# Attention with a maxima pass 20 slots ahead instead of 16, and the row of maxima sent behind exponential tile 13 instead of 17

## The chip, the cores and the metric

One core of a Trainium2 chip runs the whole program. The metric is the device time of one execution in microseconds (us), the median of several runs. TensorE is PE, VectorE is DVE, ScalarE is ACT, GpSimd is POOL, SyncE is SP. POOL, SP and ACT can issue DMAs; all of them run on the core's 16 DMA engines.

## The reference

The program embeds two inputs, runs an attention layer with quantised projections, and a mixture of eight experts. Both parts of the change lie in the attention's score, softmax and value steps:

```python
Q = (proj(q_weight, WQ, q_bias) * scaling).reshape(bsz, tgt, HEADS, HEAD_DIM)   # 32 heads of 16
K = proj(k_weight, WK, k_bias).reshape(bsz, tgt, HEADS, HEAD_DIM)
V = proj(v_weight, WV, v_bias).reshape(bsz, tgt, HEADS, HEAD_DIM)
attn = jnp.einsum('bqhd,bkhd->bhqk', Q, K)
probs = jax.nn.softmax(attn, axis=-1)
ctx = jnp.einsum('bhqk,bkhd->bqhd', probs, V).reshape(bsz * tgt, H)
```

There are 4 batches of 640 tokens and 32 heads, so 128 heads, each with a 640 x 640 score matrix. float32 precision is kept by splitting Q and K into three bf16 parts each; six pairs of parts of 16 rows are stacked on 96 partitions.

## The kernel before

`attend` works through 32 groups of 4 heads (group 0 to 31; in the code the group is `R * i + c` with R = 4). Every group goes through two passes over its scores.

**The first pass** finds each query's maximum. It has M1 = 26 slots. 25 of them are scores of 128 queries, one bank of 512 columns each (L1165; every fifth slot holds the last 128 keys of all four heads, L1168, four small matmuls). DVE reduces each bank to its negated maximum (L1255, L1257). The banks are three, `mbank`, so slot n waits on `s_mfree` until DVE has read the slot three back. Behind a group's last slot DVE joins the two halves (L1260, `nm`). Slot 4 of each group, TURN, is no score: it transposes the maxima of the group before (L1158), which needs that group's `nm`; DVE copies the result to `nmT` (L1242).

**Sending the row.** The second pass computes the scores the other way round, keys on partitions, and has the negated maximum added by the matmul itself: row 96 of `qs` (MROW) holds it, opposite ones in `ks`. ACT fills that row with a DMA of 5 KB (`put_max`, L1293), which waits until DVE has copied `nmT`. ACT issues it in the stream of its exponentials, behind tile PUT_AT of the group before.

**The second pass** has U2 = 25 tiles of scores (L1183, every fifth L1186), in three other banks, `sbank`. Tile 0 waits for the row's DMA (`s_nm`). ACT takes the exponential of each (L1281) into `pT`; tile n waits for the exponential three back. At the step from the fourth group of a loop round to the first of the next, two successive tiles fall on the same bank (`behind` gives a distance of 1). PE multiplies five exponential tiles at a time with the values (`add_values`, L1201), behind tiles 2, 7, 12, 17 and 22. ACT copies the finished context behind tile 3 of the next group (L1287), SP stores it (L1087).

**PE's order** is written out by hand in `group` (L1205): ahead of each second-pass tile s stands about one slot of the first pass. The list `ahead` is the rest of group g+1 from slot LEAD on, and then the first LEAD slots of group g+2. So with LEAD = 16 tiles 0 to 9 of group g go with slots 16 to 25 of g+1, and tiles 10 to 24 with slots 0 to 15 of g+2 (two at tile 24). Ahead of group 0 stand all slots of group 0 and the first LEAD slots of group 1, with no second pass beside them. In group 30, which has no g+2, a last transposition stands ahead of tile M1 - LEAD + 3.

**SP's order.** In group g SP stores group g-1's context and loads group g+3: six pieces each of `qs` and `ks` (L1079) and one `vs` (L1082, 320 KB), into one of four buffers. Slot 0 of a group waits for all 13 (`s_ld`). In the last two groups SP stores group 30's context, reloads context and sums, issues eight broadcasts of inverted sums (L167), and then stores group 31's context; the block ends when that has landed.

**POOL** meanwhile splits the experts' weights into bf16 halves, one of 24 pieces per group, from `SPLIT_PACE`: a load of 1 MB from memory (L1124), a cast, a subtraction, a store of 1 MB (L1140). The last piece is done in group 23.

Of the kernel before, what the change touches and what calls it, by code (L numbers as in the profile page):

```python
# [98 lines left out]
def early_fusion_kernel(nc, a, out):  # L99
    ctx = ExitStack()  # L100
    with ctx:
# [62 lines left out]
        def load_inverses(sp, b):  # L164
            for i in range(IT):
                at = (b * IT + i) * (HEADS // IT)
                sp.dma_start(den[:, b % 2, i], d_sum[at:at + HEADS // IT].unsqueeze(1).broadcast_to([HEADS // IT, HD, T])  # L167
                             ).then_inc(s_ctx[b], 16)

        attend(nc, a, locals())  # L170
        route(nc, a, locals())
        middle.close()
# [811 lines left out]
def attend(nc, a, g):  # L984
# [22 lines left out]
    PIECES = [(0, 512), (512, T - 512)]  # L1007
    CTX_AT = 3
    LAG = 3
    LEAD = 16  # L1010
    PUT_AT = 17
    R = 4
    NI = NG // R
    SPLIT_PACE = 5
# [1 line left out]
    with ctx:  # L1016
# [128 lines left out]
        def _(pe):  # L1145
            def first_pass(i, c, slot, static=False, turn=TURN):


                u, n, d = c % R, M1 * num(i, c) + slot, behind(first_bank, M1, c, slot)
                if not static or n >= d:  # L1150
                    pe.wait_ge(s_mfree, n - d + 1)
                out = ps[:, first_bank(c, slot)]
                if slot == turn:
                    if static and c == 0:
                        pe.transpose(out[0:GH * KT, 0:P], ident[:, 0:GH * KT], ident[:]).then_inc(s_m, 1)
                        return
                    pe.wait_ge(s_nmr, num(i, c))
                    pe.transpose(out[0:GH * KT, 0:P], nm[(c - 1) % 2][:], ident[:]).then_inc(s_m, 1)  # L1158
                    return
                if slot == 0:  # L1160
                    pe.wait_ge(s_ld[u], 16 * LOADS * (i + c // R + 1))
                qt, h = divmod(slot - (slot > TURN), U1)
                q = slice(qt * P, (qt + 1) * P)
                if h < GH:
                    mm = pe.matmul(out, qs[u][0:STACK, h, q], ks[u][0:STACK, h, 0:512], start=True, stop=True)  # L1165
                else:
                    for h in range(GH):
                        mm = pe.matmul(out[:, h * REST:(h + 1) * REST], qs[u][0:STACK, h, q], ks[u][0:STACK, h, 512:T],  # L1168
                                       start=True, stop=True)
                mm.then_inc(s_m, 1)  # L1170
# [34 lines left out]
            def group(i, c, static=False, following=2):  # L1205

                ahead = [(c + 1, slot) for slot in range(LEAD, M1)] if following >= 1 else []
                ahead += [(c + 2, slot) for slot in range(LEAD)] if following >= 2 else []
                for s in range(U2):
                    for cc, slot in ahead[s * M1 // U2:(s + 1) * M1 // U2]:  # L1210
                        first_pass(i, cc, slot)
                    if following == 1 and s == M1 - LEAD + 3:
                        first_pass(i, c + 2, 0, turn=0)
# [11 lines left out]
            for slot in range(M1):  # L1225
                first_pass(0, 0, slot, static=True)
            for slot in range(LEAD):
                first_pass(0, 1, slot, static=True)
# [44 lines left out]
        def _(act):  # L1273
# [9 lines left out]
            def copy_context(i, c):  # L1283
                u = c % 2
                act.wait_ge(s_pv, KT * (num(i, c) + 1) + 1)
                act.wait_ge(s_ost[u], 16 * (R // 2 * i + c // 2) + 1)
                act.copy(osb[u][:], pv[:, 0:T]).then_inc(s_oev, 1)  # L1287

            def put_max(i, c, at=TURN):

                u = c % 2
                act.wait_ge(s_mfree, M1 * (num(i, c) + 1) + at + 1)
                act.dma_start(qs[c % R][MROW:MROW + 1].rearrange("p h (k t) -> p (h k) t", k=KT),  # L1293
                              nmT[u][:]).then_inc(s_nm[u], 16)

            def group(i, c, first=False, put=TURN):
                for s in range(U2):
                    exps(i, c, s)
                    if s == CTX_AT and not first:
                        copy_context(i, c - 1)  # L1300
                    if s == PUT_AT and put is not None:
                        put_max(i, c + 1, at=put)
# [622 lines left out]
```

## Time and profile before

| | |
|---|---|
| median of 3 runs | 1871.68 us (1866.7 to 1874.78) |
| profiled execution | 1869.23 us, its span 1867.4 us |
| busy share of the span | PE 75%, DVE 70%, ACT 41%, POOL 27% |
| granted TensorE clock, mean | 0.859 |
| attention, first score of the first pass to last context copy | about 434 to 1076 us |
| experts, on the chain that ended last | 1375 us to the end |

A span is from the first to the last instruction of the profiled execution. "Idle before <-releaser" gives an engine's idle time ahead of an instruction and what ended it; an idle time of PE with the releaser "DMA qs<-nmT" is a second pass that waited for its row of maxima. Timelines merge instructions of one kind that follow each other; a row's length is that of their union. An engine name with a q (ACTq, SPq) is a DMA issue on that engine's instruction stream. The granted clock is 1.00 at 2.4 GHz and 0.50 at 1.2 GHz.

### The profile page before, as it was taken

What the parts mean: (1) busy time and instruction counts of PE and PEld (TensorE: products, weight loads), DVE (VectorE), ACT (ScalarE), POOL (GpSimd) and SP (SyncE); (2) the same over time, 40 slices, a digit from 0 to 9 for tenths busy, and PEclk for the clock granted to TensorE, in tenths of its full rate; (3) what the DMA queues carried; (4) which work ended last, traced back from release to release, by engine and by line L of the source; (5) the groups of instructions that cost most, each with busy time, mean ns of one, the idle gap of its engine ahead of it and who ended that gap; (6) DMA issues with size and microseconds to landing.
All of it is one profiled execution on the core that took longest, in us unless ns stands there. A gap on an engine that the chain in (4) does not pass through costs nothing. (4 is left out here: it accounts for less than half of the span.)

```text
span 1867.4 us, 30349 instructions
## 1 busy us (share of the span) xinstructions
PE 1396.8 (75%) x10245; PEld 783.8 (42%) x10245; DVE 1302.6 (70%) x2158; ACT 767.8 (41%) x1459; POOL 510.8 (27%) x325
## 2 busy tenths in 40 slices
PE   0365128746999999999999914359549999999993
PEld 0344013311433444444444301034537777777772
DVE  7976889987877888888888457885534444444441
ACT  4474002330666777777777700011203333333331
POOL 4000114653333434333200002324112333233321
PEclk9987558875999999999999965565569999999997
DMA  4002003779466676767554332001547887888865
GB/s 142 1 1 82 0 1 103 223 229 209 113 190 183 183 216 180 205 187 206 141 106 78 113 113 62 28 1 57 198 196 261 261 269 262 272 286 267 261 171 135
DMA packets 112867, 289.02 MB, mean 155 GB/s; under 512 B 19566, under 2 KB 54126, under 8 KB 102650
## 3 DMA queue, kind: packets, MB, share of 16 engines
q1 hardware_dynamic: 89154, 205.74, 35.7%
q0 software_dynamic: 22592, 79.70, 15.6%
q10 hardware_dynamic: 1056, 2.79, 0.5%
q8 instruction: 32, 0.52, 0.1%
q14 instruction: 33, 0.27, 0.0%
HBM read 201.17 MB, written 92.08 MB: 157 GB/s over the span
## 5 line engine op out<-in xcount | busy, mean ns | idle before, releaser
L1281 ACT ACTIVATE pT<-p 128x512 f32<-128x512 f32 x800 | 421.6, 607 | 173.8 <-PE p L1183 171.5
L1255 DVE TENSOR_REDUCE mxa<-p 128x1 f32<-128x512 f32 x640 | 409.3, 681 | 102.9 <-PE p L1165 102.8
L1165 PE MATMUL p<-ks,qs 96*128 96x512 bf16 x640 | 254.1, 400 | 30.8 <-DMA vs<-d_v 29.1
L1183 PE MATMUL p<-qs,ks 128*128 128x512 bf16 x640 | 246.2, 385 | 31.5 <-DMA qs<-nmT 19.9
L1201 PE MATMUL p<-pT,vs 128*32 128x128 f32 (+1 forms) x2560 | 207.5, 442 | 1.0 <-ACT pT L1281 1.0
L1786 PE MATMUL p<-x,w 128*128 128x256 bf16 x1728 | 191.6, 273 | 0.0
L1786 PEld LDWEIGHTS p<-x,w 128*128 128x128 bf16 x1728 | 169.1, 98 | 23.4
L1757 POOL DMA_INDIRECT d_acc<-yo,slot_row x54 | 86.7, 1606 | 311.5 <-DMA d_acc<-yo,slot_row 248.5
L1865 DVE SCALAR_TENSOR_TENSOR sg<-p,b,sg 128x256 f32<-128x256 f32 x108 | 52.2, 483 | 121.3 <-ACT sg L1831 121.2
L1201 PEld LDWEIGHTS p<-pT,vs 128*32 128x32 f32 x2560 | 67.1, 109 | 153.1 <-issue 110.3
L1136 POOL CAST xT<-xT 128x2048 bf16<-128x2048 f32 x24 | 45.3, 1887 | 303.4 <-PE p L1201 292.2
L1165 PEld LDWEIGHTS p<-ks,qs 96*128 96x128 bf16 x640 | 62.2, 97 | 141.4 <-DVE mxa L1255 46.6
L1831 ACT ACTIVATE sg<-p,b1s 128x256 f32<-128x256 f32 x108 | 51.2, 474 | 170.8 <-PE p L1786 170.8
L1257 DVE TENSOR_REDUCE mxb<-p 128x4 f32<-128x512 f32 x160 | 108.7, 680 | 0.4 <-PE p L1168 0.4
L1786 PE MATMUL p<-x,shared 128*128 128x256 bf16 x864 | 97.7, 276 | 0.8 <-ACT x L1823 0.8
L1138 POOL TENSOR_TENSOR xT<-xT 128x2048 bf16<-128x2048 f32 x24 | 97.7, 4072 | 2.0
L1798 PE MATMUL p<-w,y 128*128 128x512 bf16 x432 | 96.2, 379 | 0.0
L1183 PEld LDWEIGHTS p<-qs,ks 128*128 128x128 bf16 x640 | 62.6, 98 | 73.7 <-ACT pT L1281 35.5
L1836 ACT CAST y<-yf 128x256 bf16<-128x256 f32 x108 | 43.7, 404 | 117.6 <-DVE yf L1868 117.6
L1786 PEld LDWEIGHTS p<-x,shared 128*128 128x128 bf16 x864 | 85.3, 99 | 13.6 <-ACT x L1823 1.1
L1880 DVE SCALAR_TENSOR_TENSOR yo<-p,slot_prob,b2p 128x512 f32<-128x512 f32 x54 | 38.0, 746 | 65.0 <-PE p L1798 65.0
L1871 DVE TENSOR_TENSOR y<-yf,y 128x256 bf16<-128x256 f32 x108 | 46.0, 426 | 50.9 <-ACT y L1836 50.9
(335 smaller groups left out, 2189.5 us busy)
## 6 DMA issues: line engine op xcount, KB each, us to landing
w<-d_w SPq DMA_DIRECT2D x18, 2048.0 KB, 8.5
d_w<-xT POOLq DMA_DIRECT2D x24, 1024.0 KB, 6.5
shared<-d_w SPq DMA_DIRECT2D x9, 2048.0 KB, 8.2
w<-d_w SPq DMA_DIRECT2D x18, 1024.0 KB, 7.4
xT<-in_w1T POOLq DMA_DIRECT2D x16, 1024.0 KB, 10.8
qs<-d_q SPq DMA_DIRECT2D x192, 80.0 KB, 3.6
ks<-d_k SPq DMA_DIRECT2D x192, 80.0 KB, 3.6
d_v<-xT SPq DMA_DIRECT2D x20, 512.0 KB, 4.4
```

The costliest lines, as they stand in the source:

```text
L1138: pool.tensor_tensor(lo, wf[u], hi, ALU.subtract).then_inc(s_wsp, 1)
L1165: mm = pe.matmul(out, qs[u][0:STACK, h, q], ks[u][0:STACK, h, 0:512], start=True, stop=True)
L1183: mm = pe.matmul(out, ks[u][:, h, k], qs[u][:, h, 0:512], start=True, stop=True)
L1201: mm = pe.matmul(pv[rows, at:at + n], vs[u][:, kt, rows], src[:, col:col + n], start=kt == 0, stop=kt == KT - 1, tile_position=(0, 32 * h))
L1255: dve.tensor_reduce(mxa[u][:, h, qt:qt + 1], bank, AX.X, ALU.max, negate=True).then_inc(s_mfree, 1)
L1257: dve.tensor_reduce(mxb[u][:, :, qt], bank.rearrange("p (h k) -> p h k", h=GH), AX.X, ALU.max, negate=True).then_inc(s_mfree, 1)
L1281: act.activation(dst, ps[:, second_bank(c, s)], ACT.Exp).then_inc(s_p, 1)
L1757: pool.indirect_dma_start(d_acc, bass.IndirectOffsetOnAxis(slot_row[:, j:j + 1], 0), yo[j % OUTS][:], None, compute_op=ALU.add).then_inc(s ...
L1786: mm = pe.matmul(out, w[c][:, k, ws, t, cols], x[c][:, t, xs], start=t == 0 and m == 0, stop=t == IT - 1 and m == 2)
L1798: mm = pe.matmul(ps[:, 6 + q], y[c][:, t, ys, q * P:(q + 1) * P], w[c][:, 2, ws, t], start=t == 0 and m == 0, stop=t == IT - 1 and m == 2)
L1831: act.activation(sg[o % 2][:], ps[:, 2 + o, 0:UNIT], ACT.Sigmoid, scale=1.702, bias=b1s[c][:, 0, o:o + 1]).then_inc(s_sg, 1)
L1865: dve.scalar_tensor_tensor(sg[o % 2][:], gate, b1[c][:, 0, o:o + 1], sg[o % 2][:], ALU.add, ALU.mult).then_inc(s_u, 1)
```

## The change

Two constants. `LEAD`, the number of first-pass slots of group g+2 that stand in group g, goes from 16 to 20. `PUT_AT`, the exponential tile behind which ACT issues the row's DMA, goes from 17 to 13.

```diff
     CTX_AT = 3
     LAG = 3
-    LEAD = 16
-    PUT_AT = 17
+    LEAD = 20
+    PUT_AT = 13
     R = 4
```

Through LEAD the tiles 0 to 5 of group g now go with slots 20 to 25 of g+1 and tiles 6 to 24 with slots 0 to 19 of g+2. No instruction is added or removed; DVE's, SP's and POOL's own orders stay as they were.

PE, second group of the attention's loop body (c = 1), around the transposition of the maxima (L1158). L1165 and L1168 are first-pass slots, L1183 and L1186 second-pass tiles, L1201 the values; the REGISTER_ALU rows compute what a semaphore is compared with. Before, tiles 13 (row 320) to 15:

```order
316 L1201 MATMUL p<-pT,vs 32x128 x4
317 L1151 REGISTER_ALU
318 L1165 MATMUL p<-ks,qs 128x512
319 L1176 REGISTER_ALU
320 L1183 MATMUL p<-qs,ks 128x512
321 L1151 REGISTER_ALU
322 L1158 MATMUL p<-ident,nm 20x128
323 L1176 REGISTER_ALU
324 L1186 MATMUL p<-qs,ks 128x128 x4
325 L1151 REGISTER_ALU
326 L1168 MATMUL p<-ks,qs 128x128 x4
```

After, tiles 8 (row 298) to 10 (row 306):

```order
295 L1201 MATMUL p<-pT,vs 32x128 x4
296 L1165 MATMUL p<-ks,qs 128x512
297 L1176 REGISTER_ALU
298 L1183 MATMUL p<-qs,ks 128x512
299 L1151 REGISTER_ALU
300 L1165 MATMUL p<-ks,qs 128x512
301 L1176 REGISTER_ALU
302 L1186 MATMUL p<-qs,ks 128x128 x4
303 L1151 REGISTER_ALU
304 L1158 MATMUL p<-ident,nm 20x128
305 L1176 REGISTER_ALU
306 L1183 MATMUL p<-qs,ks 128x512
```

The transposition stood ahead of tile 14 and stands ahead of tile 10, one run of values (that behind tile 12) earlier.

ACT, first group of the loop body, around the row's DMA (L1293). Before, exponentials 16, 17 and 18:

```order
204 L1281 ACTIVATE pT<-p 128x512
205 L1279 REGISTER_ALU
206 L1281 ACTIVATE pT<-p 128x512
207 L1292 ISA
208 L1293 DMA qs<-nmT 1x20x128
209 L1279 REGISTER_ALU
210 L1281 ACTIVATE pT<-p 128x512
```

After, exponentials 12, 13 and 14:

```order
195 L1281 ACTIVATE pT<-p 128x512
196 L1279 REGISTER_ALU
197 L1281 ACTIVATE pT<-p 128x512
198 L1292 ISA
199 L1293 DMA qs<-nmT 1x20x128
200 L1279 REGISTER_ALU
201 L1281 ACTIVATE pT<-p 128x512
```

The ISA row is the wait for `nmT`. The DMA stood behind the last exponential ahead of a run of values and stands behind the first exponential after one.

PE ahead of group 0: slots of group 1 and the first tile of the second pass. Before:

```order
196 L1165 MATMUL p<-ks,qs 128x512 x4
197 L1168 MATMUL p<-ks,qs 128x128 x4
198 L1165 MATMUL p<-ks,qs 128x512
199 L1183 MATMUL p<-qs,ks 128x512
200 L1165 MATMUL p<-ks,qs 128x512
```

After:

```order
196 L1165 MATMUL p<-ks,qs 128x512 x4
197 L1168 MATMUL p<-ks,qs 128x128 x4
198 L1165 MATMUL p<-ks,qs 128x512 x4
199 L1168 MATMUL p<-ks,qs 128x128 x4
200 L1183 MATMUL p<-qs,ks 128x512
```

Four more slots (three on L1165, one on L1168) stand ahead of the first second-pass tile.

## Rows read from the trace of the kernel before

**Rows 1.** Stretches: length, busy PE, PEld, DVE, ACT, POOL, clock, DMA share, GB/s

```profile
500.00:600.00 100.00, 91.50 (x795) 39.69 (x795) 79.99 (x134) 67.65 (x129) 36.54 (x20) 0.98 0.68 187
...
900.00:1000.00 100.00, 98.26 (x873) 42.90 (x869) 85.06 (x146) 73.33 (x140) 6.67 (x4) 1.00 0.54 111
```

**Rows 2.** Waits of PE, 485 to 1050 us: us in total, times, longest

```profile
PE p L1183 <- DMA qs<-nmT: 16.6, 18, 2.2
PE p L1183 <- ACT pT L1281: 8.5, 34, 0.5
```

**Rows 3.** Timeline of PE, one group: start us, us, what, [idle before <-releaser]

```profile
700.28 0.39 PE L1183 MATMUL p<-qs,ks 128*128 128x512 bf16 x1 [0.47 <-DMA qs<-nmT]
...
704.02 0.38 PE L1165 MATMUL p<-ks,qs 96*128 96x512 bf16 x1
...
707.50 0.38 PE L1165 MATMUL p<-ks,qs 96*128 96x512 bf16 x1
...
710.58 0.27 PE L1158 MATMUL p<-ident,nm 128*20 128x128 f32 x1
...
712.05 0.38 PE L1183 MATMUL p<-qs,ks 128*128 128x512 bf16 x1
...
719.11 0.39 PE L1183 MATMUL p<-qs,ks 128*128 128x512 bf16 x1 [0.44 <-DMA qs<-nmT]
```

**Rows 4.** Timeline of ACT, the same group

```profile
710.78 2.06 ACT L1281 ACTIVATE pT<-p 128x512 f32<-128x512 f32 x4 [0.97 <-PE p L1183]
712.56 0.73 ACTq L1293 DMA_DIRECT2D qs<-nmT  x1
712.71 0.63 ACT L1281 ACTIVATE pT<-p 128x512 f32<-128x512 f32 x1
```

**Rows 5.** Timeline of SP, the same group, the last two loads

```profile
710.54 1.12 SPq L1079 DMA_DIRECT2D ks<-d_k  x1
711.84 0.88 SPq L1082 DMA_DIRECT2D vs<-d_v  x1
```

**Rows 6.** Timeline of POOL, the same group, the load of an expert's weights

```profile
709.76 0.78 POOL L1124 DMA_DIRECT2D xT<-in_w2T  x1
```

**Rows 7.** Tile view of vs, 485 to 1050 us, its last line

```profile
DMA to landing us min/median/max: 4.3/8.2/9.4
```

**Rows 8.** Timeline of PE, first scores of groups 1, 23, 24 and 28

```profile
481.47 0.38 PE L1183 MATMUL p<-qs,ks 128*128 128x512 bf16 x1
...
909.27 0.38 PE L1183 MATMUL p<-qs,ks 128*128 128x512 bf16 x1
...
928.45 0.39 PE L1183 MATMUL p<-qs,ks 128*128 128x512 bf16 x1 [0.47 <-ACT pT L1281]
...
1003.20 0.39 PE L1183 MATMUL p<-qs,ks 128*128 128x512 bf16 x1 [0.47 <-ACT pT L1281]
```

**Rows 9.** Timeline of PE, first scores of groups 4 and 7

```profile
542.57 0.39 PE L1183 MATMUL p<-qs,ks 128*128 128x512 bf16 x1 [2.17 <-DMA qs<-nmT]
...
603.41 0.38 PE L1183 MATMUL p<-qs,ks 128*128 128x512 bf16 x1 [1.94 <-DMA qs<-nmT]
```

**Rows 10.** Stretch behind group 4's start (columns as in Rows 1)

```profile
543.40:546.80 3.40, 3.40 (x20) 0.73 (x19) 1.10 (x2) 1.28 (x3) 0.24 (x1) 0.50 0.00 0
```

**Rows 11.** Timelines of PE, DVE and ACT ahead of the first group

```profile
458.03 0.61 PE L1165 MATMUL p<-ks,qs 96*128 96x512 bf16 x1
461.88 0.61 PE L1183 MATMUL p<-qs,ks 128*128 128x512 bf16 x1 [3.24 <-DMA qs<-nmT]
...
456.10 2.46 DVE L1255 TENSOR_REDUCE mxa<-p 128x1 f32<-128x512 f32 x4
...
452.62 1.36 ACTq L1293 DMA_DIRECT2D qs<-nmT  x1
```

**Rows 12.** Timelines of ACT and SP, last two groups

```profile
1060.18 0.69 ACT L1287 COPY osb<-p 128x640 f32<-128x640 f32 x1
...
1077.59 1.26 SPq L1087 DMA_DIRECT2D d_o<-osb  x1
```

## The prediction

> **What bounds the kernel now.** I read the view by stretches first. Between 500 and 600 us PE is busy 91.5 of 100 us, between 900 and 1000 us 98.3; DVE 80 to 85, ACT 68 to 73 [rows 1]. PE sets the pace of the attention, so the question is what its idle time waits for. The view of waits answers: from 485 to 1050 us PE stood 16.6 us in 18 waits on the DMA of the row of maxima, up to 2.2 us at a time, and 8.5 us in 34 waits on ACT's exponentials [rows 2]. The timelines then show one such wait from its cause: in group 12, which starts at 700.28, the transposition runs at 710.58 and ACT issues the DMA at 712.56; the next group's first score starts at 719.11, when the row is in [rows 3, 4]. That is 6.55 us from issue to use. SP's last two loads and POOL's 1 MB load are issued at 710.54, 711.84 and 709.76, just ahead of the row [rows 5, 6].
>
> **What a wait is really worth.** The 16.6 us can't be taken as the gain, since a group that doesn't wait meets other limits. The trace holds such groups: 24 to 27, behind POOL's last piece. They run from 928.45 to 1003.20, 74.75 us or 18.69 each, and none waits for the row [rows 8]. Groups 1 to 22 run from 481.47 to 909.27, 427.8 us or 19.45 each [rows 8]. If each took 18.69, they would take 411.2, a gain of 16.6 us. This agrees with the waits only by way of three corrections. Every fourth group starts with a wait of 0.47 us on ACT, since its tile 0 falls on the bank of the tile before [rows 8]. In four of the 18 waits (ahead of groups 4, 8, 12 and 20) the row's hides this, so 1.9 us of it stay. Behind the two longest waits, of 2.17 us and 1.94 us, the granted clock fell to 1.2 GHz for 3.4 us each; the stretch behind the first is shown [rows 9, 10]. Half speed for 3.4 us costs up to 1.7 us, so some 3.2 us come on top if these waits go. And a group that starts without a pause has DVE a little behind, which the total absorbs. 16.6 - 1.9 + 3.2 is 17.9; I take the 16.6 that the unwaiting groups give.
>
> **The change part by part.**
> *The row, four tiles earlier.* PUT_AT alone would put the DMA's wait ahead of the transposition; LEAD moves the transposition from tile 14 to tile 10, so it is still three tiles ahead of the issue. Exponentials 13 to 16 started at 710.78, and the DMA at 712.56, 0.15 us ahead of exponential 17 at 712.71, which had already been handed over [rows 4]. Behind exponential 13 the same DMA starts at about 710.78 - 0.15 = 710.63, 1.9 us earlier. The first score was ready to run 0.44 us before 719.11 [rows 3]. So an issue 1.9 us earlier covers every wait up to 1.9 us even if the way of the DMA doesn't get shorter; of the 18 only the 2.17 and the 1.94 leave a rest, 0.3 us together. It is also ahead of the 320 KB of `vs` in time, not behind it [rows 5], which should rather shorten the way. What is late next is the next group's tile 0 behind its own exponentials and DVE, the pace of groups 24 to 27. Gain 16 to 17 us.
>
> *A rule on queues.* From issue to use the row took 6.55 us beside SP's and POOL's loads [rows 3, 4]. The Trainium skill, DMA: Bandwidth & Descriptors, section "Queues, rings and completion order", has each DMA engine serve its queues in turn, packet by packet. By that the way would hang on the traffic of the moment and not on SP's backlog, and an issue 1.9 us earlier would land about 1.9 us earlier. The sum would be the same; only a way longer by 1.9 us would undo it, which is a rival below.
>
> *The cost in ACT's stream.* The issue takes 0.73 us [rows 4]. Today it stands ahead of a pause: exponential 18 waits for PE, which adds values. Behind exponential 13 it stands in a run of five. There the exponentials follow each other in (2.06 - 0.60) / 3 = 0.49 us [rows 4], 0.60 being one alone. Exponential 14 started at 711.27 and would now start behind 710.63 + 0.73 = 711.36, say 711.45, and end at 712.05. PE's tile 17 needs its bank and started at 712.05 [rows 3]. So the cost is 0 to 0.1 us a group, up to 3 us in 30. I take 1. The far bound is the issue ahead of the first group, 1.36 us [rows 11]: 0.6 us more a group, 18 us. I stay near 0.73, since that row repeats in all of the other groups.
>
> *Slot 0 of a group, four tiles earlier.* It waits for the group's loads. It stands ahead of tile 6 now, 704.02 - 700.28 = 3.74 us into the group, where it stood ahead of tile 10, at 7.22 [rows 3]. The last load of that group is issued at 711.84 and lands 8.2 us later (9.4 at most), at 720.0 [rows 5, 7]. With groups of 18.4 us slot 0 comes at 700.28 + 18.4 + 3.74 = 722.4. That leaves 2.4 us, at the longest landing 1.2. I cost it at nothing; the cover is thin, and a rival has its price.
>
> *DVE.* It joins the maxima behind slot 25, now in the run of tiles 3 to 7 and not 8 to 12. One reduction takes 0.61 us in a run (2.46 us for four, 0.68 for one alone [rows 11]), a run of five and the join 3.6 us, about what PE takes for five tiles, five slots and the values (707.50 - 704.02 = 3.48 [rows 3]). Nothing or some tenths, either way.
>
> *Ahead of group 0.* Four more slots stand there, 2.4 us at DVE's 0.61. PE idled 3.24 us there for its first row, after its last slot [rows 11]. The four slots fit in, 0 to 0.3 us. Group 30 has four slots less beside its second pass, and is held by ACT for most of its tiles: 0.3 to 0.9 us less; I take 0.4.
>
> *Behind the attention.* The end is a chain on SP: the copy of group 30's context at 1060.18, its store, the sums and their broadcasts, and group 31's store at 1077.59 [rows 12]. It starts with group 31's tile 3, so what the groups before save comes through whole. The experts' part is not touched.
>
> **The sum**, against the profiled execution's own time: 1869.2 - 16.6 (groups 1 to 22) - 0.4 (group 30) + 1.0 (ACT) = 1853.2, a gain of 16.0 us, 0.86%. The profiled execution lies 2.45 us under the median of the runs, 1871.68. Against the median: 1855.7. The forecast's own range is 1849 to 1862: the gain of 16.6 with the far corrections (17.9, 0.9 for group 30, a higher clock in group 0, some run-to-run difference) below, a third of the waits left above.
>
> **The rivals.**
> 1. *The row's landing doesn't come earlier.* If what lets it in is the moment at which SP's and POOL's traffic has gone, then an earlier issue only waits longer. For it: the way is 6.5 us beside that traffic, and the start at 719.11 is near the landing of `vs` at 720.0 [rows 3, 5, 7]. Against it: the row is 5 KB and would now stand ahead of `vs`. With half of the gain lost the time is 1863, with all of it 1871.
> 2. *ACT's issue blocks its run.* SP's issues stretch to 1.12 us and 0.88 us just when the row would now be issued [rows 5]. If ACT's stretches alike, to 1.36 us [rows 11], tile 17 comes 0.6 us late in each of 30 groups: 18 us against 17, 1873. Against it: today's issue overlaps SP's stretched one of 711.84 to 712.72 and takes 0.73 [rows 4, 5].
> 3. *Slower: slot 0 waits for its loads.* Place: PE, ahead of tile 6. It decides from a landing of over 8.2 + 2.4 = 10.6 us. Each us over that costs 22 us in 22 groups, so that from 11.8 us on the kernel is slower than before. A landing of 12 us gives 1.4 x 22 = 31 us against 17: 1886, and more if such pauses bring the clock down. Against it: no such landing between 485 and 1050 us took over 9.4 [rows 7].
> 4. *The change does nothing at the wait*, since `nmT` isn't ready when ACT comes to issue. Today transposition and issue are 2.0 us apart, and in the new order there is a run of values more between them, which makes it safer. 1871.
>
> **How the numbers follow.** Forecast 0.66; rival 1 0.14; rival 2 0.12, of which 0.02 slower by over 0.5%; rival 3 0.05; rival 4 and the rest 0.03. 0.5% is 9.4 us, about what a measurement of this kernel can tell from no change. Faster by over that, below 1862.3: nearly all of the forecast and a little of rivals 1 and 2, 0.67. Slower by over it: 0.07. Within: 0.26. The range takes in the forecast's own and reaches over the two milder rivals: 1849 to 1872.
>
> **What the profile after would show.** The waits of PE on `qs<-nmT` gone or under 2 us in all; waits on ACT near 9 us, with 0.47 us at each fourth group's start; four groups in a row in about 74.8 us, with or without POOL's traffic; no stretch at 1.2 GHz between 480 and 1050 us. Rival 1 shows as waits on that DMA that stay; rival 2 as an issue over 0.73 us and waits ahead of tile 17; rival 3 as waits of PE's L1165 on `vs<-d_v`. The attention should end some 16 us earlier, and the rest should take as long as before. The forecast is wrong if groups without the row's wait take 19.2 us or more.

## The result, and the profile after

The changed kernel takes 1958.22 us in the median of 4 runs (1956.14 to 1961.38), the kernel before beside it 1869.19 us (1864.51 to 1874.78). The ratio is 1.0476, with a 95% interval of 1.0441 to 1.0512: 4.8% slower, where 0.9% faster was forecast. The profiled execution took 1959.49 us, its span 1957.7.

The waits of PE from 485 to 1130 us, the attention without its first and last group (us in total, times, longest), answer to [rows 2]:

```profile
PE p L1165 <- DVE mxa L1255: 58.2, 30, 2.6
PE p L1183 <- ACT pT L1281: 9.4, 36, 0.5
```

The row of maxima is gone from the list, as forecast. In its place PE's first pass waits for DVE. The stretches (length, busy us of PE, PEld, DVE, ACT, POOL, granted clock, DMA share, GB/s) answer to [rows 1]:

```profile
500.00:600.00 100.00, 87.30 (x685) 35.74 (x697) 83.49 (x118) 61.51 (x114) 29.18 (x16) 0.93 0.56 157
...
900.00:1000.00 100.00, 85.00 (x676) 35.06 (x685) 85.59 (x116) 60.92 (x112) 34.75 (x18) 0.95 0.56 150
```

PE fell from 91.5 and 98.3 to 87.3 and 85.0. DVE looks as busy as before, with 118 instructions in 100 us where it had 134: something takes longer. The page's list of costly groups has it, a line that was too small for that list before (busy us, mean ns, idle before):

```profile
L1260 DVE TENSOR_TENSOR nm<-mxa,mxb 128x20 f32<-128x20 f32 x32 | 92.0, 2875 | 1.1
```

This is the join of the two halves of the maxima, 20 elements a lane. The view of that line from 485 to 900 us gives its durations (ns min/median/max), the first row of the kernel before, the second of the kernel after:

```profile
L1260 DVE TENSOR_TENSOR nm<-mxa,mxb x22: 180/579/589, 489.9 to 898.7; 128x20 f32<-128x20 f32 x22
```

```profile
L1260 DVE TENSOR_TENSOR nm<-mxa,mxb x18: 3886/3892/3900, 486.7 to 880.0; 128x20 f32<-128x20 f32 x18
```

The timeline after, one group, shows what it stands beside:

```profile
717.40 4.07 POOL L1138 TENSOR_TENSOR xT<-xT 128x2048 bf16<-128x2048 f32 x1
717.61 3.89 DVE L1260 TENSOR_TENSOR nm<-mxa,mxb 128x20 f32<-128x20 f32 x1
...
722.16 0.39 PE L1165 MATMUL p<-ks,qs 96*128 96x512 bf16 x1 [2.37 <-DVE mxa L1255]
```

POOL's subtraction runs from 717.40 to 721.47, the join from 717.61 to 721.50. It starts just behind the subtraction and ends with it. PE, which may be three slots ahead of DVE, runs dry and waits 2.37 us. Before, in group 12, the same two instructions hardly met:

```profile
704.83 4.07 POOL L1138 TENSOR_TENSOR xT<-xT 128x2048 bf16<-128x2048 f32 x1
```

```profile
708.36 0.58 DVE L1260 TENSOR_TENSOR nm<-mxa,mxb 128x20 f32<-128x20 f32 x1
```

The subtraction ended at 708.90, so the join started 0.54 us ahead of that end.

ACT's issue of the row, with the exponential ahead of it and the run behind it, answers to [rows 4]:

```profile
704.39 0.60 ACT L1281 ACTIVATE pT<-p 128x512 f32<-128x512 f32 x1 [1.16 <-PE p L1183]
704.49 0.73 ACTq L1293 DMA_DIRECT2D qs<-nmT  x1
705.42 2.07 ACT L1281 ACTIVATE pT<-p 128x512 f32<-128x512 f32 x4 [0.43 <-PE p L1183]
```

The issues also mark the groups. Four groups from the timeline of ACT, first after, then before:

```profile
659.15 0.73 ACTq L1293 DMA_DIRECT2D qs<-nmT  x1
...
751.35 0.73 ACTq L1293 DMA_DIRECT2D qs<-nmT  x1
```

```profile
655.39 0.73 ACTq L1293 DMA_DIRECT2D qs<-nmT  x1
...
731.39 0.73 ACTq L1293 DMA_DIRECT2D qs<-nmT  x1
```

After: 92.20 us, 23.05 a group. Before: 76.00 us, 19.00 a group. SP's last chain answers to [rows 12]:

```profile
1147.16 0.34 SPq L1087 DMA_DIRECT2D d_o<-osb  x1
...
1162.69 0.85 SPq L1087 DMA_DIRECT2D d_o<-osb  x1
...
1178.04 0.40 SPq L1400 DMA_DIRECT2D wTo<-in_o_wT  x1
```

Group 31's store stands at 1162.69, 85.1 us later than at 1077.59, so nearly all of the 90.3 us by which the span grew lies in the attention. The last row is the next block's first load; it stood at 1090.32 before and comes 87.7 us later. Where the 5 us behind the attention arise was not followed.

### The profile page after: what moved, and what is told of

The parts are those of the page before. It is cut to its first block and busy times, and to the rows that moved or that the text cites. A ratio compares the mean times of both kernels' runs of the same rounds, so it can differ in the third digit from the quotient of the medians.

```text
span 1957.7 us, 30230 instructions
## 1 busy us (share of the span) xinstructions
PE 1428.8 (73%) x10126; PEld 787.5 (40%) x10245; DVE 1379.7 (70%) x2158; ACT 780.0 (40%) x1459; POOL 513.9 (26%) x325
## 5 line engine op out<-in xcount | busy, mean ns | idle before, releaser
L1281 ACT ACTIVATE pT<-p 128x512 f32<-128x512 f32 x800 | 433.9, 606 | 246.7 <-PE p L1183 104.8
L1165 PE MATMUL p<-ks,qs 96*128 96x512 bf16 x640 | 254.1, 407 | 94.9 <-DVE mxa L1255 59.3
L1183 PE MATMUL p<-qs,ks 128*128 128x512 bf16 x560 | 223.3, 399 | 14.6 <-ACT pT L1281 12.2
L1201 PE MATMUL p<-pT,vs 128*32 128x128 f32 (+1 forms) x2560 | 219.3, 462 | 2.0 <-ACT pT L1281 2.0
L1165 PEld LDWEIGHTS p<-ks,qs 96*128 96x128 bf16 x640 | 62.5, 98 | 212.4 <-DVE mxa L1255 132.7
L1201 PEld LDWEIGHTS p<-pT,vs 128*32 128x32 f32 x2560 | 69.0, 113 | 167.0 <-issue 122.0
L1260 DVE TENSOR_TENSOR nm<-mxa,mxb 128x20 f32<-128x20 f32 x32 | 92.0, 2875 | 1.1
L1183 PEld LDWEIGHTS p<-qs,ks 128*128 128x128 bf16 x640 | 63.9, 100 | 45.6 <-ACT pT L1281 35.2
```

What stands on the lines that cost most here:

```text
L1183: mm = pe.matmul(out, ks[u][:, h, k], qs[u][:, h, 0:512], start=True, stop=True)
L1201: mm = pe.matmul(pv[rows, at:at + n], vs[u][:, kt, rows], src[:, col:col + n], start=kt == 0, stop=kt == KT - 1, tile_position=(0, 32 * h))
L1260: dve.tensor_tensor(nm[u][:], mxa[u][:].rearrange("p h k -> p (h k)"), mxb[u][:].rearrange("p h k -> p (h k)"), ALU.min).then_inc(s_nmr, 1)
L1281: act.activation(dst, ps[:, second_bank(c, s)], ACT.Exp).then_inc(s_p, 1)
```

## The theories

**Theory J.** The join has two inputs in SBUF. It can't run while POOL's instruction reads SBUF, and is held until that ends. LEAD = 20 moved it from behind tile 9 to behind tile 5, into POOL's subtraction. Before, it met only the last 0.54 us of that, which made it 0.58 us long against 0.18 when free. The Trainium skill, SBUF — State Buffer, section "Who interferes with whom", states it: "A DVE instruction with two SBUF inputs contends with a GpSimd instruction that reads SBUF". The trace after agrees, 3.89 us beside a POOL instruction of 4.07.

**Rival S.** The order of the slots itself makes DVE late, whatever POOL does. **Rival A.** The row's DMA in ACT's run of exponentials carries the loss. **Rival H.** Any DVE instruction at this place would be held.

**Theory P**, formed behind the first runs: an issue on ACT costs what stands behind it in a run of exponentials, and nothing ahead of a pause.

## Experiments

The diffs are against the changed kernel, or against the changed kernel without a join where that is said. Those of "half of the change" and "the second part alone" are against the kernel before.

### The lead alone

```diff
     LEAD = 20
-    PUT_AT = 13
+    PUT_AT = 17
```

> The lead alone: 20 slots, the row still sent behind tile 17. After the change DVE's join of the maxima (L1260) takes 3.89 us in a group in place of 0.58, since it starts beside POOL's subtraction (L1138, 4.07 us) and ends with it. Theory J (the join is held until POOL's subtraction ends, and the lead is what moved it there): about 1958 us, the join again near 3.9 us. Rival A (the row's DMA in ACT's run of exponentials, PUT_AT = 13, carries the loss): under 1890. The row would be sent late enough that the DMA waits of before could come back, but groups are longer by the hold, so under J none.

Measured: 1944.55 us, ratio to before 1.0406 (1.0388 to 1.0425). The join takes 3.89 us again:

```profile
L1260 DVE TENSOR_TENSOR nm<-mxa,mxb x32: 178/3891/3899, 449.8 to 1120.1; 128x20 f32<-128x20 f32 x32
```

The lead carries 76 of the 89 us; rival A falls as the main cause. The expectation of 1958 was 13.5 us too high: the issue behind tile 13 has a cost of its own. The groups behind POOL's last piece show it without the hold. Four of them take 75.01 us here, from issue to issue, or 18.75 each, and 76.10 us or 19.03 each with tile 13. That is 0.28 us a group, 8.4 us in 30. The clock also fell less often behind the held joins, 15 times in 23 groups and 18 times with tile 13; at up to 1.7 us a fall that is up to 5 us more.

### Half of the change

```diff
-    LEAD = 16
-    PUT_AT = 17
+    LEAD = 18
+    PUT_AT = 15
```

> Half of the change: 18 slots and tile 15. The join starts some 0.9 to 1.8 us later in the group than with 20 slots, so less of POOL's 4.07 us is left. Theory J: the join takes about 2 to 3 us in groups with POOL's work, PE's waits on DVE near 1 us each and no half-speed stretches, the time between 1880 and 1925. Rival S (the order of the slots itself makes DVE late, whatever POOL does): the join short, the loss about half of 89 us, near 1914, without long joins.

Measured: 1894.15 us, ratio 1.0138 (1.0119 to 1.0157). Its timeline, and PE's waits from 485 to 1060 us:

```profile
711.38 4.07 POOL L1138 TENSOR_TENSOR xT<-xT 128x2048 bf16<-128x2048 f32 x1
```

```profile
712.79 2.70 DVE L1260 TENSOR_TENSOR nm<-mxa,mxb 128x20 f32<-128x20 f32 x1
```

```profile
PE p L1165 <- DVE mxa L1255: 34.6, 23, 1.5
```

The join starts 1.41 us into the subtraction, and ends with it again (715.49 and 715.45). Its length is what is left of POOL's instruction. PE's waits are 1.5 us at most, and the granted clock stayed at 1.00 between 600 and 700 us.

### The changed kernel, POOL's work later in the group

```diff
-                pool.wait_ge(s_pv, SPLIT_PACE * n + 1)
+                pool.wait_ge(s_pv, SPLIT_PACE * n + 3)
```

> The changed kernel with POOL's pieces released two value steps later (behind the values of tiles 10 to 14 and not of the group before), so that cast and subtraction fall some 7 us later in the group, clear of the join. Theory J: the join takes 0.18 us, no PE waits of 2.4 us on DVE, no half-speed stretches, and the time comes to what was forecast for the change, 1850 to 1862. Rival S: the time stays near 1958.

Measured: 1862.63 us, ratio 0.9965 (0.9954 to 0.9977). The join takes 0.18 us in every group, and PE's waits on DVE are 2.5 us in all. Moving POOL's work alone, with the order of the slots untouched, took 96 us away. Rival S falls. The time lies 0.6 us above the expected range of 1850 to 1862; the issue behind tile 13 is still in it.

### The changed kernel without a join

```diff
...
-                    pe.wait_ge(s_nmr, num(i, c))
-                    pe.transpose(out[0:GH * KT, 0:P], nm[(c - 1) % 2][:], ident[:]).then_inc(s_m, 1)
+                    pe.wait_ge(s_mfree, M1 * num(i, c))
+                    for at, half in enumerate((mxa, mxb)):
+                        mm = pe.transpose(out[0:GH * KT, at * P:(at + 1) * P],
+                                          half[(c - 1) % 2][:].rearrange("p h k -> p (h k)"), ident[:])
+                    mm.then_inc(s_m, 1)
...
-                dve.tensor_copy(nmT[(c - 1) % 2][:], ps[0:GH * KT, first_bank(c, slot), 0:P]).then_inc(s_mfree, 1)
+                both = ps[0:GH * KT, first_bank(c, slot), 0:2 * P].rearrange("r (a p) -> r p a", a=2)
+                dve.tensor_reduce(nmT[(c - 1) % 2][:], both, AX.X, ALU.min).then_inc(s_mfree, 1)
...
-                dve.wait_ge(s_mfree, base + M1)
-                dve.tensor_tensor(nm[u][:], mxa[u][:].rearrange("p h k -> p (h k)"),
-                                  mxb[u][:].rearrange("p h k -> p (h k)"), ALU.min).then_inc(s_nmr, 1)
```

> The changed kernel without the join: PE transposes both halves of the maxima into one bank and DVE takes the minimum of the two from PSUM as it copies them, so that no DVE instruction of the loop has two SBUF inputs. POOL's work stays where it is. Theory J (the hold is on DVE's instruction with two SBUF inputs while POOL reads and writes SBUF): no DVE instruction of the loop over 0.7 us, the time 1850 to 1862. Rival H (any DVE instruction at this place would be held while POOL subtracts): a reduction takes 3.9 us in its place, and the time stays near 1958.

Measured: 1862.98 us, ratio 0.9965 (0.9951 to 0.9978), 1.0 us above theory J's range and far from rival H's 1958. POOL's subtraction stands where it stood (line numbers of this kernel; the reduction of the maxima is L1260 here):

```profile
714.92 4.07 POOL L1138 TENSOR_TENSOR xT<-xT 128x2048 bf16<-128x2048 f32 x1
715.01 1.28 DVE L1260 TENSOR_REDUCE mxa<-p 128x1 f32<-128x512 f32 x2
717.12 1.29 DVE L1260 TENSOR_REDUCE mxa<-p 128x1 f32<-128x512 f32 x2 [0.83 <-PE p L1169]
```

Reductions from PSUM run through it at their usual 0.6 us. Rival H falls: at the same place the join is held and a reduction from PSUM isn't. This run doesn't show that it takes two SBUF inputs. The trace of the kernel before has a case with one, further on in the attention's output stage: a copy of 64x5 elements from SBUF to SBUF (ns min/median/max).

```profile
L1551 DVE COPY qgtok_ctx<-qgb_ctx x8: 151/1081/1110, 1152.6 to 1289.1; 64x5 f32<-64x5 f32 x8
```

Two of the eight run without a neighbour, in 0.15 and 0.17 us. The other six take 1.08 to 1.11 us, and each ends 0.02 to 0.03 us behind an instruction of POOL on SBUF (L1439).

### Without the join, the row ahead of a pause

```diff
-    PUT_AT = 13
+    PUT_AT = 12
```

> The changed kernel without the join (both halves transposed, minimum taken from PSUM), and the row's DMA behind tile 12, the last exponential ahead of a pause. In the run with tile 13 the step from exponential 13 to 14 is 0.94 us where it was 0.49, and the pause behind tile 17 only 1.38 where it is 1.60: 0.25 to 0.3 us a group. Theory P (the issue costs what stands behind it in a run, and nothing ahead of a pause): 30 x 0.28 = 8 us less than the same kernel with tile 13 (1862.98), so 1853 to 1857, groups at 18.3, 18.6, 18.8 and 19.3 us in turn. Rival (the missing part of the forecast gain is the slots' order itself): 1861 to 1865.

Measured: 1855.57 us, ratio 0.9939 (0.9922 to 0.9955). This and the kernel with both faults mended by moving work (1856.04, below) are the fastest. Theory P holds: 7.4 us against the kernel with tile 13, 8 expected. Four groups, from 659.66 to 734.67, take 75.01 us or 18.75 each:

```profile
659.66 0.73 ACTq L1295 DMA_DIRECT2D qs<-nmT  x1
...
734.67 0.74 ACTq L1295 DMA_DIRECT2D qs<-nmT  x1
```

In the stretch from 600 to 700 us PE is busy 97.86 us at a clock of 1.00; no wait on `qs<-nmT` is left:

```profile
600.00:700.00 100.00, 97.86 (x873) 43.55 (x866) 83.19 (x139) 72.65 (x140) 40.92 (x23) 1.00 0.77 198
```

### The second part alone

```diff
     LEAD = 16
-    PUT_AT = 17
+    PUT_AT = 13
```

> The second part alone: 16 slots, the row behind tile 13. The transposition stands ahead of tile 14, so ACT stops behind exponential 13 until DVE has copied the row, some 0.8 us later, then issues for 0.73 us. Theory P: exponential 14 comes 1.1 to 1.4 us late, PE loses about 1 us in each of 30 groups, and the waits for the row mostly go (16 us): 1875 to 1895. Theory J: the join stays at 0.58 us. If PUT_AT were free, 1852 to 1860.

Measured: 1885.9 us, ratio 1.0097 (1.008 to 1.0114). ACT's timeline, and PE's waits from 485 to 1050 us:

```profile
710.78 0.60 ACT L1281 ACTIVATE pT<-p 128x512 f32<-128x512 f32 x1 [0.97 <-PE p L1183]
711.55 0.73 ACTq L1293 DMA_DIRECT2D qs<-nmT  x1
712.40 2.07 ACT L1281 ACTIVATE pT<-p 128x512 f32<-128x512 f32 x4 [1.02 <-DVE mxb L1257]
```

```profile
PE p L1183 <- ACT pT L1281: 34.2, 65, 1.1
```

ACT stands until DVE has the row copied, at 711.52, and exponential 14 starts 1.62 us behind 13 where 0.49 is usual. The waits for the row are gone here too, and more came in their place. Each of the two constants alone makes the kernel slower.

### The changed kernel, a copy in place of POOL's subtraction

```diff
-                pool.tensor_tensor(lo, wf[u], hi, ALU.subtract).then_inc(s_wsp, 1)
+                pool.tensor_copy(lo, wf[u]).then_inc(s_wsp, 1)
```

> The changed kernel with POOL's subtraction replaced by a plain copy of the same size (the experts' weights lose their low halves, so the last stage works on other numbers; its times don't depend on them). It asks which POOL instruction holds the join. The copy has one SBUF input and takes about 1.9 us, so POOL computes until some 6.4 us into the group, and the join comes at about 5. If only an instruction with two inputs holds it: join 0.18 us, 1861 to 1865. If any POOL instruction does: join 1 to 2 us, PE loses less than 0.5 us a group, 1864 to 1874. Near 1958 would speak against theory J altogether.

Measured: 1880.8 us, ratio 1.0077 (1.006 to 1.0094), above both expected ranges. The join against POOL's two instructions:

```profile
700.42 1.89 POOL L1136 CAST xT<-xT 128x2048 bf16<-128x2048 f32 x1 [14.54 <-PE p L1201]
702.37 1.89 POOL L1138 CAST xT<-xT 128x2048 bf16<-128x2048 f32 x1
```

```profile
702.60 1.70 DVE L1260 TENSOR_TENSOR nm<-mxa,mxb 128x20 f32<-128x20 f32 x1
```

The second copy ends at 704.26, the join at 704.30. A POOL instruction with one SBUF input holds the join as well. Held for 1.5 us a group the kernel loses 18 us against the one with POOL's work moved (1862.63), about 0.8 us in each of 23 groups, more than the 0.5 us that I had allowed; which of the small delays behind the hold makes up the rest wasn't taken apart. Some waits for the row also came back, 3.7 us in all.

### The kernel before without the join

> The kernel before (16 slots, tile 17) without the join. It asks what the join's 0.58 us cost before, and whether the row's wait is what the forecast priced. Theory J: 0.4 us less on DVE in 22 groups, mostly hidden; the waits for the row stay: 1860 to 1870, waits on the row 10 to 20 us in all. The difference to the same kernel with 20 slots (1862.98 with tile 13) is then the gain of the lead without the hold.

The edit is that of the kernel without a join, on 16 slots and tile 17. Measured: 1869.44 us, ratio 1.0005 (0.9991 to 1.0019). PE's waits from 485 to 1050 us:

```profile
PE p L1187 <- DMA qs<-nmT: 14.9, 16, 2.6
```

The join's 0.58 us cost nothing that can be measured before; the interval of the ratio is 2.6 us wide to either side. The waits for the row are still there, so it is the earlier row, sent ahead of a pause, that gives the 13.9 us between this kernel and the one with 20 slots and tile 12.

### The two faults mended by moving work alone

```diff
-    PUT_AT = 13
+    PUT_AT = 12
...
-                pool.wait_ge(s_pv, SPLIT_PACE * n + 1)
+                pool.wait_ge(s_pv, SPLIT_PACE * n + 3)
```

> The changed kernel with both faults mended by moving work alone: POOL's pieces two value steps later, the row's DMA behind tile 12. Theories J and P together: the join at 0.18 us, the step from exponential 13 to 14 back at 0.49, and the time of the kernel without the join and with tile 12 (1855.57), 1853 to 1858. If the join had a cost of its own beside the hold, it would show here as a difference of some us.

Measured: 1856.04 us, ratio 0.9933 (0.9902 to 0.9963), the same as without a join. Two numbers turn the change from a loss of 89 us into a gain of 12.

### 24 slots

```diff
-    LEAD = 20
-    PUT_AT = 13
+    LEAD = 24
+    PUT_AT = 7
```

> The kernel without the join with 24 slots and the row behind tile 7, again ahead of a pause. It asks whether the third rival of the forecast, slot 0 waiting for its group's loads, has a place at all. Slot 0 stands ahead of tile 2 here, some 0.9 us into the group; the group's last load lands 19.7 to 20.4 us after the start of the group before, in which it was issued, and groups take 18.75. So PE should wait for `vs<-d_v` some 0.3 to 1 us in each of 22 groups: 1860 to 1880. If no such wait shows, 1853 to 1858.

This is on the kernel without the join. Measured: 1874.85 us, ratio 1.0028 (1.001 to 1.0047). PE's waits from 485 to 1045 us:

```profile
PE p L1169 <- DMA vs<-d_v: 14.7, 18, 2.0
```

The third rival of the forecast exists, four slots further on. Its waits are 14.7 of the 19.3 us that this kernel is slower than the one with 20 slots and tile 12. The rest isn't the loads': the groups behind POOL's last piece have no such wait and take 18.91 us in place of 18.75. With 20 slots no run showed such a wait.

## Why the prediction was wrong

**Where the 85 us in the attention come from.** The sum, from the runs:

| term | us a group | groups | us |
|---|---|---|---|
| the row four tiles earlier (19.45 before [rows 8], 18.75 without join and with tile 12) | -0.70 | 22 | -15.4 |
| the issue behind tile 13 in place of 12 (19.03 and 18.75) | +0.28 | 30 | +8.4 |
| the join held by POOL (23.05 and 19.03, after and without join) | +4.02 | 23 | +92.5 |
| sum | | | +85.5 |

Group 31's store came 85.1 us later. That the sum comes so near is partly chance: it leaves out what differs ahead of group 0, up to 1 us, and in the last groups. The 19.03 is the mean of four groups of the kernel without a join and with tile 13, which take 18.56, 18.87, 19.17 and 19.50 us in turn from exponential 0 to exponential 0.

**The step that failed is the one on DVE**: "It joins the maxima behind slot 25, now in the run of tiles 3 to 7 and not 8 to 12. ... Nothing or some tenths, either way." It took the join's duration as its own, and the term stood in the sum at nothing. In its place the runs showed a join that is held until POOL's subtraction ends, 3.89 us in place of 0.58, at a cost of 4.02 us in each of 23 groups. The forecast counted work and left out what else runs at the new place. The trace of before had what was needed: the join took 0.58 us beside POOL and 0.18 us behind POOL's last piece; group 12's join stood at 8.1 us into the group, and POOL's subtraction from 4.5 to 8.6. Slot 25 moved to about 5 us. The text worked that out for DVE's queue and never laid it beside POOL's timeline. None of the four rivals names it. The forecast's own sign of being wrong, groups of 19.2 us or more without the row's wait, did appear, with 23.05.

**How the hold turns into 4.02 us.** The join comes 3.89 - 0.18 = 3.71 us late. PE waits 2.37 of it, and loses some more in small delays: in the one group of four in which the clock didn't fall, the hold costs 2.80 (21.97 us against 19.17). In the other three, in which the clock fell behind the wait, it costs 4.25 to 4.57. The stretch behind a wait without a fall, and the one behind a wait with it:

```profile
700.50:704.00 3.50, 3.40 (x32) 1.33 (x31) 2.82 (x6) 2.27 (x4) 0.65 (x1) 1.00 0.99 268
722.50:726.00 3.50, 3.50 (x18) 1.17 (x19) 2.88 (x6) 2.39 (x4) 0.61 (x1) 0.57 0.95 253
```

Both waits were 2.4 us long; of the 23 such waits, 2.37 to 2.59 us, 18 were followed by a fall. A stretch of 3.4 us at half speed costs up to 1.7 us, as priced in the forecast [rows 10]; it came behind the new waits, not the old ones. The length of the wait alone doesn't decide it: in the kernel before without the join PE waited 2.62 us for the row ahead of 501.77, and the granted clock was 1.00 from 500 to 600 us. A granted clock of 0.93 to 0.95 over 100 us is 10 to 14 us at 1.2 GHz.

**ACT's issue: right mechanism, wrong size.** The term was 0 to 0.1 us a group with 1 us taken; it is 0.28, 8.4 us in all. The forecast had the DMA start 0.15 us ahead of exponential 13, as it had stood ahead of 17. But 17 had been handed over early, in a run, and 13 is the first behind a pause. It starts when PE's scores arrive, and the DMA only 0.10 us behind it (704.39 and 704.49). Exponential 14 then starts 0.94 us behind 13 in three of four groups, and 1.03 in the fourth, which is the one shown (705.42), in place of 0.49. That is a delay of 0.45 us or more, where 0.18 was assumed (711.45 for 711.27). No issue of the loop was stretched: 0.73 to 0.77 us, so rival 2's reason did not occur.

**What was right.** The waits for the row went, all of them, and their worth: 16.6 us were forecast from groups of 18.69 us, and 15.4 us came, with groups of 18.75. Rival 1 falls: the waits are also gone in the four kernels whose groups take 18.75 to 19.03 us beside POOL's traffic. Rival 4 falls too: `nmT` was ready at 702.13 and ACT issued at 704.49. Group 0's first exponential came 1.0 us later (464.90 against 463.86) where 0 to 0.3 was said; in the other kernels with 20 slots it came at 462.55 to 465.51, so a cost of the four slots ahead of group 0 can't be told from that. SP's chain passed nearly all of the delay on: group 31's first exponential came 86.3 us later (1143.83 against 1057.55), its store 85.1. A kernel with both faults mended takes 1855.6 to 1856.0 us. That this is the forecast's 1855.7 is partly luck, since it has no cost on ACT and a little less gain from the row.

## What to carry to other kernels

Before an instruction is moved in time, list what the other engines do at its new place, above all whether VectorE and GpSimd both work on SBUF there; a short instruction that everything waits for is worth a look at its minimum and its maximum duration, since a gap between them can be a wait that no view of waits lists. Put a DMA issue behind the last instruction ahead of an engine's pause, not behind the first after one. A price taken from a stretch without the neighbour's traffic holds only if the neighbour is absent at the new place too.

## What the runs showed of the hardware

A DVE instruction with two SBUF inputs was held for as long as a POOL instruction on SBUF ran, with one input (1.70 us beside a copy of 1.89) as with two (3.89 beside 4.07), and the hold counts as DVE's busy time. A DVE copy with one SBUF input was held too (L1551, 0.15 us free, up to 1.11 us beside POOL). Reductions from PSUM weren't held. All of these POOL instructions read and write SBUF, so no run shows which of the two holds DVE.

POOL's subtraction wasn't slowed: 4.07 us before and after. In each of these cases it had started first. Where DVE started at the same time, the trace of the kernel before shows POOL held, in an earlier stage:

```profile
300.00 1.40 POOL L867 TENSOR_TENSOR xT<-xT,xn 128x640 f32<-128x640 f32 x1 [1.52 <-ACT xn L847]
303.04 2.08 POOL L867 TENSOR_TENSOR xT<-xT,xn 128x640 f32<-128x640 f32 x1 [1.64 <-ACT xn L847]
```

```profile
303.04 0.82 DVE L969 TENSOR_TENSOR xT<-xT,BT 128x640 f32<-128x640 f32 x1
```

DVE's instruction, with two SBUF inputs, took its usual 0.82 us, and POOL's took 2.08 in place of 1.40.

Waits of PE of 1.5 us left the clock at 2.4 GHz. Behind waits of 2.4 us it fell 18 times in 23 with tile 13 and 15 times in 23 with tile 17, and behind the one wait of 2.62 us it didn't fall.
